# Projection with stacked halves, DMA transposes on one queue and unrolled programs in an AdaLN feed-forward kernel

## What is computed

```python
w = weights[conditions]                     # (64, 64, 64)
z = einsum('bct,bcd->bdt', x, w)            # projection
def hbitlinear(x, w, bits):                 # fwht: normalized Walsh-Hadamard transform
    xq = act_quant(fwht(x), bits)           # absmax of each row, 8 bits, dequantized
    wq = weight_quant(w)                    # ternary, scale is the mean of |w|
    return einsum('bsd,fd->bsf', xq, wq)
h = hbitlinear(z, w_up, 8)                  # 512 -> 1024
h = square(relu(h))
out = x + hbitlinear(h, w_down, 8)          # 1024 -> 512
```

## Time and profile before

| | us |
|---|---|
| runs | 285.24, 287.08, 282.93; median 285.24 |
| profiled execution: span | 279.9 |
| profiled execution: time of its own | not shown by the page |
| PE busy | 246.1 (88%), 2,116 matmuls |
| PE weight loads busy | 203.6 (73%) |
| DVE busy | 204.7 (73%), 341 instructions |
| ACT busy | 147.4 (53%), 193 instructions; its 64 transposes to issue are not counted |
| POOL busy | 181.4 (65%), 231 instructions |
| HBM | 13.70 MB read, 8.39 MB written |

### The profile page before, as it was taken

One profiled execution on the slowest core, in us unless ns is written; L12 is line 12 of the kernel. 1 busy time (PEld: TensorE's weight loads), 2 busy tenths in 40 slices (PEclk: granted clock), 3 DMA queues, 4 the chain that ended last, 5 costly groups with the idle time before them and its releaser, 6 DMA issues.

```text
span 279.9 us, 6739 instructions
## 1 busy us (share of the span) xinstructions
PE 246.1 (88%) x2116; PEld 203.6 (73%) x2116; DVE 204.7 (73%) x341; ACT 147.4 (53%) x193; POOL 181.4 (65%) x231
## 2 busy tenths in 40 slices
PE   0266899799999999999999999999999899985872
PEld 0266797797979797979797888888888687754441
DVE  0145557799888697888878796969697977887632
ACT  2143588765647465655656565556462766641220
POOL 1333133869797979697979788887976467278510
PEclk9999999999999999999999999999999999998899
DMA  6865963245563745585664437434443325553364
GB/s 188 305 210 204 191 158 51 42 122 95 143 107 92 154 122 89 143 143 128 155 191 87 122 75 215 94 94 98 116 84 106 81 57 109 135 112 75 75 86 141
DMA packets 67369, 34.96 MB, mean 125 GB/s; under 512 B 57490, under 2 KB 57618, under 8 KB 67346
## 3 DMA queue, kind: packets, MB, share of 16 engines
q10 hardware_dynamic: 52432, 14.75, 28.4%
q1 hardware_dynamic: 14914, 19.93, 23.3%
HBM read 13.70 MB, written 8.39 MB: 79 GB/s over the span
## 4 chain that ended last, share of the span: by engine, by line
PE 61%; issue 9%; DMA 8%; POOL 6%; DVE 5%; ACTq 4%; ACT 3%; SPq 2%; POOLq 0%; DVEq 0%
PE u_ps L750 15%; PE h_ps L737 14%; PE o_ps L761 13%; PE y_ps L708 10%; PE z_ps L721 8%; DMA zqT<-zq 4%; POOL p L422 4%; ACTq L527 2%; DMA uqT<-uq 2%; ACT uq L547 2%; POOL u_deq L430 1%; DVE u_max L931 1%; ACTq L554 1%; DVE y L893 1%; DMA w_pair<-in_L_cond_weights_dram 1%
## 5 line engine op out<-in xcount | busy, mean ns | idle before, releaser
L422 POOL TENSOR_TENSOR p<-g 128x512 f32<-128x512 f32 x64 | 80.9, 1287 | 23.6 <-DVE g L924 22.9
L750 PEld LDWEIGHTS u_ps<-had_sb,p 128*128 128x128 f32 x512 | 61.0, 193 | 12.2 <-POOL p L422 7.1
L750 PE MATMUL u_ps<-had_sb,p 128*128 128x128 f32 x512 | 63.8, 278 | 6.8 <-POOL p L422 4.4
L737 PE MATMUL h_ps<-zqT,w_upT 128*128 128x256 f16 x512 | 61.8, 272 | 2.5 <-ACT g L534 1.3
L761 PE MATMUL o_ps<-w_downT,uqT 128*128 128x512 f16 x256 | 61.7, 384 | 2.4 <-DMA uqT<-uq 2.4
L385 POOL TENSOR_TENSOR x_half<-x_all 128x512 f32<-128x512 f32 (+1 forms) x32 | 40.9, 1300 | 25.9 <-PE y_ps L708 15.3
L737 PEld LDWEIGHTS h_ps<-zqT,w_upT 128*128 128x128 f16 x512 | 49.4, 98 | 9.5 <-issue 2.0
L547 ACT ACTIVATE uq<-u_ps,u_mul 128x1024 f16<-128x1024 f32 x32 | 35.6, 1114 | 34.2 <-DVE u_mul L944 28.2
L534 ACT ACTIVATE g<-h_ps 128x512 f32<-128x512 f32 x64 | 37.7, 595 | 21.8 <-PE h_ps L737 10.1
L931 DVE TENSOR_REDUCE u_max<-u_ps 128x1 f32<-128x1024 f32 x32 | 39.0, 1218 | 10.8 <-PE u_ps L750 10.7
L708 PE MATMUL y_ps<-w_pair,x_half 64*128 64x64 f32 x512 | 35.4, 293 | 12.1 <-DMA w_pair<-in_L_cond_weights_dram 12.1
(11 more groups left out here) (35 smaller groups left out, 142.1 us busy)
## 6 DMA issues: line engine op xcount, KB each, us to landing
x_all<-in_x_dram SPq DMA_DIRECT2D x32, 256.0 KB, 3.3
out_dram<-out_sb SPq DMA_DIRECT2D x32, 256.0 KB, 2.3
w_raw<-in_L_ffn_w_up_dram ACTq DMA_DIRECT2D x4, 512.0 KB, 4.4
w_raw<-in_L_ffn_w_down_dram SPq DMA_DIRECT2D x4, 512.0 KB, 4.9
w_pair<-in_L_cond_weights_dram SPq DMA_DIRECT2D x64, 16.0 KB, 2.2
zqT<-zq ACTq DMA_TRANSPOSE x32, 2.7
uqT<-uq ACTq DMA_TRANSPOSE x32, 3.1
had_sb<-in_hadamard_dram ACTq DMA_DIRECT2D x1, 64.0 KB, 3.6
```

The lines of the kernel that those rows point to most:

```text
L422: nc.gpsimd.tensor_tensor(new[:, :, m, :], old[:, :, 0, :], old[:, :, 1, :], (ALU.add, ALU.subtract)[m]).then_inc(s_p8[k], 1)
L737: mm = nc.tensor.matmul(h_ps[u % 2][:, i, :], w_upT[:, q, f * P:(f + 1) * P], zqT[par][:, q, :], start=(q == 0), stop=(q == TC - 1))
L750: mm = nc.tensor.matmul(u_ps[:, c * P:(c + 1) * P], p8[par][:, c, k * P:(k + 1) * P], had_sb[:, :], start=True, stop=True)
```

## The change

All sixteen tiles are written out for every engine; no loop and no register addresses but for the table's index remain. What changes in the stages:

- x is loaded with its two halves stacked: rows 0 to 63 hold a sample's first 256 columns, rows 64 to 127 the last 256. A matrix w of the table is loaded onto both halves of the rows; ACT writes a second copy with the sign of rows 64 to 127 turned (sign_w). One matmul with 128 rows and 128 moving columns then gives sum and difference at once. x_outer is gone. project comes in two parts, l = 0 and 1, of four matmuls each, waited for apart.
- x is loaded a second time in the old layout for the residual (load_xn, 512 KB a tile), into a ring of four. x_all is gone.
- turn_z is one DMA a tile. It and turn_u are issued by SyncE, as all other DMAs but those of the indices and the Hadamard matrix.
- Scale columns are kept for all tiles, so keep_z is gone and token_units is two instructions. y_odd, zq and out_sb are double, zqT is six deep.
- For k = 1 of the last two tiles had_u writes h_ps and down writes z_ps.
- The weights' stages and the arithmetic stay as they are.

```diff
-x_v = x.rearrange("(j two) c t -> (two c) j t", two=2)
+x_v = x.rearrange("(t b) c (h n) -> h c t b n", b=BT, h=2)      # BT = 4; xn_v: the old view
+xs: 6 x [P, BT, 256]; ws: 8 x [P, BT, 2, C]; xn: 4 x [P, KP, T]; zq: 2 x [P, KP, T]; zqT: 6 x [P, KP, TC, P]
...
-    def load_x(t, half, par, j):
-        if j == 0:
-            after(sp, s_x[par], XLOADED * half)
-        pair = KP * t + j
-        sp.dma_start(x_all[:, pair:pair + 1, :], x_v[:, pair:pair + 1, :]).then_inc(s_x[par], 16)
+    def load_x(t):
+        for l in range(2):
+            after(sp, s_y[l], t - NX + 1)
+        for h in range(2):
+            sp.dma_start(xs[t % NX][h * C:(h + 1) * C, :, :], x_v[h, :, t, :, :]).then_inc(s_x[t % NX], 16)
-    def gather_w(t, half, par, j):
-        pair = KP * t + j
-        if j == 0:
-            after(sp, s_wc[par], LOADED * half)
-        after(sp, s_y, t - 3 if t < 6 else t - 1)
-        sp.wait_ge(s_cond, 16)
-        for n in range(2):
-            row = sp.value_load(cond_sb[0:1, 2 * pair + n:2 * pair + n + 1], min_val=0, max_val=S_SETS - 1)
-            lo = C * n
-            sp.dma_start(
-                w_pair[t if t < 4 else par][lo:lo + C, j:j + 1, :],
-                w_cond[bass.ds(row, 1), :, :].rearrange("s c d -> c s d"),
-            ).then_inc(s_wc[par], 16)
+    def gather(t, b):
+        if b == 0:
+            sp.wait_ge(s_cond, 16)
+            for l in range(2):
+                after(sp, s_y[l], t - NW + 1)
+        if b == 0:
+            _, rows[:] = nc.values_load_multi_w_load_instructions(
+                cond_sb[0:1, BT * t:BT * t + BT], engines=[mybir.EngineType.SP], min_val=0, max_val=S_SETS - 1)
+        row = rows[b]
+        sp.dma_start(ws[t % NW][:, b, 0, :],
+                     w_cond[bass.ds(row, 1), :, :].broadcast_to([2, C, C])).then_inc(s_wc[t % NW], 16)
+    def load_xn(t):
+        for k in range(KP):
+            after(sp, s_out[k], t - NXN + 1)
+        sp.dma_start(xn[t % NXN][:, :, :], xn_v[:, KP * t:KP * t + KP, :]).then_inc(s_xn[t % NXN], 16)
-    def turn_z(t, half, par, k):
-        for u in range(4):
-            after(act, s_h[u], t - 1)
-        act.wait_ge(s_zq[k], t + 1)
-        act.sem_inc(s_turn, 1)
-        act.dma_start(zqT[par][:, :, k * P:(k + 1) * P], zq[k][:, :], transpose=True)\
-            .then_inc(s_zqT[k], 16)
+    def turn_z(t):
+        for u in range(4):
+            after(sp, s_h[u], t - NZT + 1)
+        for k in range(KP):
+            sp.wait_ge(s_zq[k], t + 1)
+        sp.sem_inc(s_turn, 1)
+        sp.dma_start(zqT[t % NZT][:, :, :, :].rearrange("p k q n -> p (k q) n"),
+                     zq[t % 2][:, :, :].rearrange("p k t -> p (k t)"), transpose=True)\
+            .then_inc(s_zqT[t % 2], 16)
+    def turn_u(t, k):
+        after(sp, s_o[k], t - 1)
+        sp.wait_ge(s_uq[k], t + 1)
+        sp.sem_inc(s_turn, 1)
+        sp.dma_start(uqT[t % 2][k][:, :, :], uq[k][:, :], transpose=True).then_inc(s_uqT[k], 16)
-        xt = x_all[:, bass.ds(t * KP, KP), :].rearrange("p j (h n) -> p j h n", h=2)
-        nc.gpsimd.tensor_tensor(x_half[h][:, :, :], xt[:, :, 0, :], xt[:, :, 1, :],
-                                (ALU.add, ALU.subtract)[h]).then_inc(s_xh[h], 1)
-    def keep_z(t, half, par):
-        ...
-    def token_units(t, half, par):
-        ...
+    def token_units(t):
+        pool.wait_ge(s_cols, 3)
+        for k in range(KP):
+            pool.wait_ge(s_zmul[k], t + 1)
+        nc.gpsimd.tensor_tensor(z_unit[:, t, :, :].rearrange("p w k -> p (w k)"),
+                                z_col[:, t, :, :].rearrange("p w k -> p (w k)"),
+                                unit4[:, :, :].rearrange("p w k -> p (w k)"), ALU.mult).then_inc(s_unit, 1)
+        pool.wait_ge(s_unit, t + 1)
+        nc.gpsimd.tensor_tensor(kappa[:, t, :, :].rearrange("p w k -> p (w k)"),
+                                z_unit[:, t, :, :].rearrange("p w k -> p (w k)"),
+                                z_unit[:, t, :, :].rearrange("p w k -> p (w k)"), ALU.mult).then_inc(s_kappa, 1)
+    def sign_w(t):
+        act.wait_ge(s_sgn, 2)
+        act.wait_ge(s_wc[t % NW], 16 * BT * (t // NW + 1))
+        nc.scalar.activation(ws[t % NW][:, :, 1, :], ws[t % NW][:, :, 0, :], ACT.Copy,
+                             scale=sgn[:, 0:1]).then_inc(s_ws, 1)
-    def project(t, half, par):
-        for h in range(2):
-            pe.wait_ge(s_xh[h], t + 1)
-        pe.wait_ge(s_wc[par], LOADED * (half + 1))
-        after(pe, s_yb, 2 * t)
-        w = w_pair[t if isinstance(t, int) and t < 4 else par]
-        for h in range(2):
-            for l in range(2):
-                for j in range(KP):
-                    for b in range(2):
-                        rows = slice(b * C, (b + 1) * C)
-                        mm = nc.tensor.matmul(y_ps[:, b, l, h, j, :],
-                                              x_half[h][rows, j, l * P:(l + 1) * P], w[rows, j, :],
-                                              start=True, stop=True)
-        mm.then_inc(s_y, 1)
+    def project(t, l):
+        if l == 1:
+            after(pe, s_yodd, t)
+        else:
+            after(pe, s_yb, 2 * t)
+        pe.wait_ge(s_x[t % NX], 32 * (t // NX + 1))
+        pe.wait_ge(s_ws, t + 1)
+        for k in range(KP):
+            for b in range(2):
+                mm = nc.tensor.matmul(y_ps[:, l, k, b, :, :].rearrange("p s d -> p (s d)"),
+                                      xs[t % NX][:, 2 * k + b, l * P:(l + 1) * P],
+                                      ws[t % NW][:, 2 * k + b, :, :].rearrange("p s d -> p (s d)"),
+                                      start=True, stop=True)
+        mm.then_inc(s_y[l], 1)
+def own_home(t, k):
+    return k == 1 and t in LAST
+def u_home(t, k):
+    return h_flat if own_home(t, k) else u_ps[:, :]
+def o_home(t, k):
+    return z_ps[:, :] if own_home(t, k) else o_ps[:, :]
...
+# SyncE's order, up to turn_u(2, 1)
+load_x(0); load_x(1); gather(0, 0); gather(0, 1); gather(0, 2); gather(0, 3); gather(1, 0)
+load_up(0); load_up(1); load_up(2); gather(1, 1); gather(1, 2); gather(1, 3); load_up(3)
+gather(2, 0); gather(2, 1); load_x(2); gather(2, 2); gather(2, 3); gather(3, 0); load_down(0)
+gather(3, 1); gather(3, 2); load_down(1); load_x(3); gather(3, 3); turn_z(0); load_down(2)
+load_down(3); gather(4, 0); gather(4, 1); load_x(4); gather(4, 2); gather(4, 3); gather(5, 0)
+load_x(5); turn_z(1); gather(5, 1); gather(5, 2); gather(5, 3); load_x(6); gather(6, 0)
+gather(6, 1); gather(6, 2); gather(6, 3); gather(7, 0); gather(7, 1); gather(7, 2); gather(7, 3)
+load_x(7); turn_z(2); load_xn(0); gather(8, 0); load_x(8); gather(8, 1); gather(8, 2); gather(8, 3)
+gather(9, 0); gather(9, 1); gather(9, 2); gather(9, 3); load_x(9); gather(10, 0); load_x(10)
+gather(10, 1); gather(10, 2); turn_z(3); turn_u(0, 0); gather(10, 3); load_xn(1); gather(11, 0)
+gather(11, 1); gather(11, 2); gather(11, 3); load_xn(2); load_xn(3); turn_u(0, 1); load_x(11)
+gather(12, 0); load_x(12); gather(12, 1); turn_z(4); gather(12, 2); gather(12, 3); gather(13, 0)
+turn_u(1, 0); store(0, 1); load_xn(4); store(0, 0); gather(13, 1); gather(13, 2); gather(13, 3)
+load_x(13); gather(14, 0); turn_u(1, 1); load_x(14); gather(14, 1); turn_z(5); gather(14, 2)
+gather(14, 3); store(1, 0); gather(15, 0); turn_u(2, 0); store(1, 1); load_xn(5); gather(15, 1)
+gather(15, 2); gather(15, 3); turn_u(2, 1)
...
+# TensorE's order, from up(15, 2)
+up(15, 2); up(15, 3); down(11, 0); down(11, 1); had_u(13, 0); down(12, 0); had_u(13, 1)
+had_u(14, 1); down(12, 1); had_u(14, 0); down(13, 0); had_u(15, 1); had_u(15, 0); down(13, 1)
+down(14, 1); down(14, 0); down(15, 1); down(15, 0)
```

More of the change, by code:

```diff
@@ L40 @@
 F = 1024
-PAIRS = B // 2
 KP = 2
 TOK = KP * P
-TILES = PAIRS // KP
+TILES = B // (2 * KP)
+BT = B // TILES
 TC = T // P
@@ L196, in after @@
         def after(eng, semaphore, count):
[L198 to L231 removed]
+            if count > 0:
+                eng.wait_ge(semaphore, count)
@@ L674, in _ @@
-            run_steps(act, begin, step, finish, 6)
+            load_cond()
+            load_had()
+            sign_w(0)
+            y_split(0)
+            weight_abs(0, 1)
+            quant_z(0, 0)
+            sign_w(1)
+            y_split(1)
+            weight_abs(0, 3)
+            quant_z(0, 1)
+            sign_w(2)
+            weight_round(0, 0)
+            weight_round(0, 1)
+            quant_z(1, 0)
+            weight_round(0, 2)
+            weight_round(0, 3)
+            y_split(2)
@@ new lines, in _ @@
+            weight_abs(1, 1)
+            sign_w(3)
+            quant_z(1, 1)
+            relu(0, 0)
+            relu(0, 1)
+            square(0, 0)
+            weight_abs(1, 3)
+            y_split(3)
+            quant_z(2, 0)
+            relu(0, 2)
+            sign_w(4)
+            relu(0, 3)
+            square(0, 1)
+            y_split(4)
+            weight_round(1, 1)
+            weight_round(1, 0)
+            relu(1, 1)
+            quant_z(2, 1)
+            sign_w(5)
```

(85 more changed lines are left out.)

1747 lines of the change are left out of this document (1058 added, 689 removed).

## The result

The changed kernel takes 312.65 us (median of 4 runs, 311.75 to 316.93), the one before 284.56 (282.93 to 287.08): ratio 1.102, 95% interval 1.096 to 1.108. It is slower, nearly by the amount forecast (314), though only half by the way that was forecast. The profiled execution spans 310.6 us (forecast 309) and took 312.39 by itself.

The account below looks back on a forecast made before the run. PE bounds the middle (229 of 279.9 us); afterwards gathers on two engines bound the start: 151 us to down(2,1), 151 of PE work left and 7 at the end make 309, plus 5.3 outside the span: 314 us, range 268 to 331.

Parts of the forecast that it names:

- the two engines' sum: DMA queue at the start: 65.5 us other transfers plus 82 us gathers, 151 us with first piece and completion.
- Step 4, two engines for a gather: Gathers at the start: outermost count 2 confines each to two engines; 64 cost 82 us instead of 10.
- Step 4, "SP itself would be earlier ... under 75 us to there": SyncE's issuing up to turn_u(2,1): gather issues 0.47 us, transposes 1.2, under 75 us, so ahead of the two engines.
- Step 4, 20 ns a piece: Price of a gather's 256-byte piece on a DMA engine: 20 ns taken, ends 10 and 24.
- A: Forecast case: two engines delay turn_z and turn_u of tiles 0 to 2; span 284 to 332; chance 0.62.
- Steps 1 and 2: Projection on 128 rows saves 2.4 us in all; kept columns, unrolling, transposes off ACT give nothing in the middle.
- both engines had idle time beside a full PE: ACT and POOL mid-kernel: removing POOL's copies and ACT's 64 issues of 1.2 us gains nothing there.
- Step 3, the start: If data come in time: first project 9.6 us, first had_u 52; 21 us of PE lost instead of 27.
- Step 3, the end: From the last up: 35.2 us to the end, 7 lost instead of 15, through own PSUM for k=1.
- B: Faster: gathers spread over 16 engines, or a piece about 10 ns; span 266, 271 us; chance 0.25.
- C: No change: pieces 12 to 14 ns, or bulk loads ahead of transposes eat B's gains; 283 us; chance 0.13.

Follow-up runs that it names:

- e9: Changed kernel with the gathers of tiles 6 to 15 and their index reads issued by ACT, still on two engines: 314.06 us, ratio 1.113.
- e7: Interleaved-rows kernel (e2) with the gathers of tiles 6 to 15 and their index reads issued by ACT: 273.57 us, ratio 0.966.
- after: The changed kernel itself, gathers on two engines and all issued by SyncE: 312.65 us, ratio 1.102 to the kernel before.
- e2: Changed kernel with the stacked halves' rows interleaved: gathers on 16 engines, one x DMA a tile; 281.95 us, ratio 0.9985.
- e4: Changed kernel with fixed table rows, so no index reads or register work for gathers: 301.6 us, ratio 1.069.
- e5: Changed kernel with the DMA transposes issued by ACT again, gathers still on two engines: 337.45 us.
- e6: Interleaved-rows kernel (e2) with the DMA transposes issued by ACT: 301.71 us; the comparison uses one run, 294.38.
- e12: e7 with ACT's gathers from tile 7 issued a tile earlier, and residual(11,1) before g_outer(15,1) on VectorE: 274.0 us, ratio 0.967.
- e8: e2 without own PSUM for k=1 of the last two tiles, and k in order 0, 1 there: 298.21 us, ratio 1.050.
- e3: Changed kernel with gathers of half the pieces, still two engines, rows 64 to 127 of w constant: 302.08 us, one run.

## Why the prediction was right, and where it was not

The direction and the first cause were right: a gather is confined to two engines, and this is a limit of the start. That the number came out within 2 us is in part luck: a second limit of the same size, SyncE's program, was priced at little more than half its length, and the two engines' sum was too long by about what the missing limit cost. The span came out 1.6 us above the forecast; the time outside it, forecast 5.3 us and measured 1.8 (312.39 less 310.6), outweighed that.

**Step 4, two engines for a gather: right, and shown.** Completion pieces say 2 for a gather, on SyncE's queue and on ACT's. The rule of the Trainium skill (DMA: Bandwidth & Descriptors, "Rules for kernel authors"), that c zero-stride copies in front confine a DMA to at most c engines, holds here. For the gather before, outermost count 64, sixteen were used. The interleaved form is worth 42.8 us with the same issuers and the same bytes (e9 to e7), or 28.8 with all on SyncE (after to e2). It halves the x issues and shortens the index reads as well, so neither figure is the price of the two engines alone.

**Step 4, "SP itself would be earlier ... under 75 us to there": wrong.** SyncE's work up to turn_u(2,1) is about 132 us, not 75. Terms left out or too small: an issue of this gather takes 0.594 us in the median and one of x 0.639, where I carried over 0.47; the mean of the 112 issues is 0.67 (75.5 us against 53); index reads 11 us, register work 12.6 and gaps of some 20 us were counted at nothing in the sum, though the same reads stood in the trace of before. The forecast still hit because the engines' sum was too long by about as much as the collision of the two costs, which is luck: the engines alone allow down(2,1) at 139 (e4), SyncE alone at some 137 (132 to the issue and the 5.5 us from there to down(2,1)), and together they give 149.7, forecast 151. As I read it, two nearly equal limits add, since an issue drawn out by a full queue is not made up later; no run separates that.

**Step 4, 20 ns a piece: too high.** 17 ns or less (e4), 14.5 where the pieces stand densest (e9). With 14.5 the forecast's sum would give the engines 129 us up to down(2,1), and e4 shows 139: either the pieces are not that dense throughout, or another term is too short. The 1.5 us for a transpose and the shares of x and the weights were not measured by themselves. Two slips in the sum are small beside that: four stores stand before turn_u(2,1), not five (0.8 us), and pieces of 14 ns with 1.34 us for 512 KB give a span of 280, not the 284 at which A's range begins.

**Steps 1 and 2.** A half projection takes 0.89 us, as forecast, POOL's half sums and copies are gone (128.6 us busy for 181.4), and PE is full in the middle. But "both engines had idle time beside a full PE" was too easy a reason for pricing the transposes' move at nothing: e5 and e6 show that on ACT's program, as I placed them, they would have cost 12 us (281.95 to the 294.38 of e6) to 22 us (spans of after and e5) in the new order. Idle share is not cover, when an issue blocks the engine at the wrong moment.

**Step 3, the start.** With gathers on 16 engines it is right (10.1 and 51.3 for 9.6 and 52). On two engines the first gathers' issue is itself held (3.67 us at the longest), ws comes later and the first project starts at 13.67; the forecast put this 4 us nowhere, and as I read it they did not matter: up(0,0) waited 4.85 us for turn_z(0) all the same. The forecast laid the first project's double length to TensorE at 1.2 GHz; the granted clock of that stretch is 1.00 in the windows of both kernels, so these rows show the double length and not its cause.

**Step 3, the end.** Forecast 35.2 us from the last up, measured 37.3. The walk missed the wait below, where g_outer(15) stands ahead of residual(11,1) on DVE (start, length; pieces of 0.05 us and less are left out):
```profile
275.88 3.90 DVE g L1190 x2
279.90 1.21 DVE u_max L1202
281.11 0.67 DVE out_sb L1220
281.82 3.35 PE o_ps L918 x8
```
PE stood idle for 2.12 us there, and the granted clock behind it was 0.53 (282 to 284 us), so that this down took 3.35 us in place of 1.7. e12 took the wait away and gained nothing clear of the spread: a wait for quantizing took its place. The gain was put at 8 us and laid to the own PSUM; e8 puts the PSUM and the order of k that goes with it at 11.8.

**The rivals.** B as written, gathers on 16 engines and then 266, would have failed even so: e2 has that, and a shorter program besides, and spans 281.8, for SyncE's program stands in the way. It needs a second issuer besides (e7, 270.6). C's time, 283, is near what e2 takes, but mainly by SyncE and not by bulk loads ahead of a transpose: transposes 1024 wide landed 3.2 and 3.3 us after their issue there in the median, against 3.1 in a queue of their own.

Left open: how the 149.7 divides between the two limits, since e3 and e4 each lift one and meet the other; what e3's single run is worth beyond a few us; and how the gain of the interleaved form divides between the engines and SyncE's shorter program.

## What to carry to other kernels

Look at the outermost count of a DMA's source before looking at its bytes: two copies in front of a matrix, cheap in the code, put a whole gather on two engines here, and the mean DMA share hid it. When several engines' DMAs are gathered into one program, add up that program instruction by instruction, index reads, register work and gaps too, at the durations of the new shapes; in this kernel moving 40 small issues and their index reads to a second engine was worth 11 us, once their shape was changed. A limit is known only when the other one has been lifted, so lift both together at least once.
